# Cross attention of a decoder layer: the second head's sum of weights moved from GpSimd to VectorE in every second block of queries

## The reference, cut to what matters

```python
scores = jnp.einsum('bqhd,bkhd->bhqk', q, k) / TEMP
attn = jax.nn.softmax(scores, axis=-1)
out = jnp.einsum('bhqk,bkhd->bqhd', attn, v).reshape(b, sq, N_HEAD * VALUE_DIM)
out = out @ Wo + bo + residual
```

## Time and profile before

| | |
|---|---|
| median of 3 runs | 1935.51 us |
| all runs | 1913.4, 1935.51, 1937.34 us |
| span of the profiled execution | 1916.1 us |
| mean granted TensorE clock | 0.952 of full speed |
| cross attention, pairs 0 to 7 | from about 640 us to the end |
| one pair, from 1 to 6 | 147.4 us |

### The profile page before, as it was taken

The page is one execution under the profiler, slowest core; times in us unless marked ns, Lnnn a source line. Parts: engine busy times, 40 slices in busy tenths (PEclk is TensorE's granted clock), DMA queues, the critical chain, the costliest instruction groups (busy, mean ns, idle before and its releaser), DMA issues.

```text
span 1916.1 us, 29762 instructions
## 1 busy us (share of the span) xinstructions
PE 1767.4 (92%) x10698; PEld 885.2 (46%) x10698; DVE 1270.0 (66%) x2503; ACT 920.3 (48%) x1866; POOL 940.8 (49%) x800
## 2 busy tenths in 40 slices
PE   7999989998988999999999999999999999999983
PEld 3544444443444544445545545544554554554431
DVE  5677777777643657756656655665665675667888
ACT  2345676666665243344454444445445444445441
POOL 1000000000001466658888888898888888882111
PEclk9867999999999899999999999999999999999996
DMA  4232113332011000000000000000000000000001
GB/s 115 34 37 35 21 16 36 36 45 55 2 34 55 11 0 1 1 11 4 1 11 4 1 10 4 1 11 1 4 11 1 4 1 1 4 11 23 1 28 38
DMA packets 29129, 34.48 MB, mean 18 GB/s; under 512 B 4290, under 2 KB 27139, under 8 KB 27523
## 3 DMA queue, kind: packets, MB, share of 16 engines
q1 hardware_dynamic: 28984, 32.59, 9.1%
HBM read 14.99 MB, written 4.19 MB: 10 GB/s over the span
## 4 chain that ended last, share of the span: by engine, by line
PE 76%; DVE 16%; ACT 4%; issue 3%; SPq 1%; DMA 1%; POOL 0%; ACTq 0%; DVEq 0%; POOLq 0%
PE psum L974 17%; PE psum L954 14%; PE psum L939 9%; DVE maxima L1247 8%; PE psum L860 8%; PE psum L772 6%; PE psum L810 4%; PE psum L835 4%; PE psum L1005 3%; PE psum L927 3%; PE psum L872 2%; PE psum L986 2%; DVE parts_room L1341 1%; DVE stack_room L1297 1%; ACT stack_room L1116 1%
## 5 line engine op out<-in xcount | busy, mean ns | idle before, releaser
L1247 DVE TENSOR_REDUCE maxima<-psum 128x1 f32<-128x400 f32 (+5 forms) x1664 | 860.1, 580 | 322.7 <-PE psum L939 211.7
L747 POOL TENSOR_TENSOR parts_room<-parts_room,weights_room 128x512 f32<-128x512 f32 (+1 forms) x565 | 706.1, 1283 | 136.3 <-ACT weights_room L1137 136.3
L1137 ACT ACTIVATE weights_room<-psum 128x512 f32<-128x512 f32 (+1 forms) x757 | 405.5, 599 | 491.2 <-PE psum L954 429.4
L1065 ACT ACTIVATE weights_room<-psum 128x512 f32<-128x512 f32 (+3 forms) x640 | 300.2, 535 | 183.4 <-PE psum L835 104.1
L1455 POOL TENSOR_SCALAR rstd<-meanvar 128x2 f32<-128x2 f32 (+1 forms) x24 | 9.8, 408 | 726.9 <-DVE meanvar L1197 726.9
L954 PE MATMUL psum<-stack_room,dk_hi 64*128 64x512 f32 (+1 forms) x1408 | 264.1, 410 | 8.1 <-ACT weights_room L1137 4.8
L939 PE MATMUL psum<-k_later,stack_room 64*128 64x400 f32 (+1 forms) x896 | 243.4, 412 | 22.3 <-DVE stack_room L1297 14.6
L939 PEld LDWEIGHTS psum<-k_later,stack_room 64*128 64x128 f32 x896 | 128.4, 184 | 220.8 <-issue 121.2
L974 PE MATMUL psum<-weights_room,parts_room 128*64 128x512 f32 (+1 forms) x754 | 203.1, 606 | 0.0
L974 PE MATMUL psum<-weights_room,late_room 128*64 128x512 f32 (+1 forms) x760 | 202.5, 605 | 0.0
L835 PE MATMUL psum<-stack_room,stack_room 51*128 51x512 f32 (+3 forms) x640 | 143.4, 448 | 34.2 <-DVE maxima L1247 31.7
(11 more groups left out here) (136 smaller groups left out, 1854.4 us busy)
## 6 DMA issues: line engine op xcount, KB each, us to landing
stack_room<-parts_room SPq DMA_DIRECT2D x84, 128.0 KB
x_block<-x_dram SPq DMA_DIRECT2D x8, 512.0 KB, 4.8
x_middle<-x_block SPq DMA_DIRECT2D x4, 512.0 KB, 3.1
x_block<-x_middle SPq DMA_DIRECT2D x4, 512.0 KB, 3.9
out_dram<-x_block SPq DMA_DIRECT2D x8, 256.0 KB, 2.1
stack_room<-parts_room SPq DMA_DIRECT2D x24, 64.0 KB
parts_room<-ctx_dram SPq DMA_DIRECT2D x1, 1536.0 KB
stack_room<-shift_rows SPq DMA_DIRECT2D x64, 2.0 KB
```

The source lines that it names most:

```text
L747: engine.tensor_tensor(sum_[:kw, :], old[:kw, :], weights[u % NP_WEIGHTS][:kw, :], ALU.add) \
L1065: engine.activation(w_self[s % NW][:, m, 0:n], bank_of(use + m)[:, 0:n], ACT.Exp, scale=SELF_SCALE).then_inc(emptied(use + m), 1)
L1137: engine.activation(weights[u % NP_WEIGHTS][:kw, :], pair_scores[u % NSCORES][:kw, :], ACT.Exp, scale=CROSS_SCALE).then_inc(pair_exp, 1)
L1247: engine.tensor_reduce(maxima[:, p % 2, i // TB, n, i % TB, ch:ch + 1], bank_of(use + n)[:, 0:real - k0], AX.X, ALU.max) \
```

## The change

In blocks 1 and 3 of pairs 0 to 6 the adds of the second head (m = 1) are VectorE's; the first head's stay with GpSimd, as do both heads' in blocks 0 and 2. That is 7 pairs x 2 blocks x 12 adds = 168 adds. GpSimd's adds stand at `pair_scores`, VectorE's at `pair_values`, so these adds also come later in the list of stages. The bookkeeping of the two semaphores follows.

```diff
+    def adds_on_vector(p, b, m):
+
+        return on_vector(p) or (b % 2 == 1 and m == 1)
...
         for m in range(HP if added_up(p, j) else 0):
-            made[on_vector(p)] += 1
-            added_made[p, b, j, m] = added_on_vector if on_vector(p) else added_on_pool, made[on_vector(p)]
+            vector = adds_on_vector(p, b, m)
+            made[vector] += 1
+            added_made[p, b, j, m] = added_on_vector if vector else added_on_pool, made[vector]
...
             elif kind == "pair_values":
                 p, b, j, s = at
                 for m in range(HP):
-                    if added_up(p, j) and on_vector(p):
+                    if added_up(p, j) and adds_on_vector(p, b, m):
                         add(dve, engine, p, b, j, s, m)
...
             elif kind == "pair_scores":
                 p, b, j, s = at
                 for m in range(HP):
-                    if added_up(p, j) and not on_vector(p):
+                    if added_up(p, j) and not adds_on_vector(p, b, m):
                         add(pool, engine, p, b, j, s, m)
```

## The result

The changed kernel took 1977.92 us (median of 4 executions, 1976.16 to 1985.25) against 1925.08 us for the kernel before: a ratio of 1.0303, with a 95% interval of 1.0256 to 1.0349. It is slower.

A forecast was written before the change was run, and what follows sets the result against it. TensorE was taken as the bound, waiting only for VectorE. 31 us of adds, 58 with the clash, plus 12 of clock made 70 us; added to the 1935.5 median, 2005 us, 3.6% slower, range 1945 to 2060.

The forecast's parts named there:

- rival 1: VectorE hides the adds except at V4: 20 us, at most 31 without meetings; 1955 to 1967 us, chance 0.27.
- GpSimd's relief: 168 GpSimd adds removed, 215 us of its time, beside TensorE's work and waited for by nobody: 0.
- the clash: VectorE adds meeting GpSimd adds in odd blocks: 0.7 us per two-add stage, raising the sum from 31 to 58 us.
- V4: Values stage of odd blocks between inversions and reductions, without a gap: in pairs 1 to 6 all 1.45 us go to TensorE.
- V3: Values stage of odd blocks, two adds: in pairs 1 to 6 cost 0 in block 1, 1.15 us in block 3.
- The sum without meetings: All odd blocks of pairs 0 to 6, if an add costs what it does in the last pair: 31 us.
- V2: Values stage of block 1, pairs 1 to 6: two adds of 1.45 us fit 2.30 us of idle time, cost 0.
- V5: Values stage of odd blocks, pairs 1 to 6: block 1 0.1 us without meetings, 0.8 with; block 3 0 without.
- V6: Values stage of odd blocks, pairs 1 to 6: cost 0 without meetings, 0.25 us in block 1 with them.
- The clock: One clock dip of 1.7 us in every second of the 14 odd blocks: 12 us, between 0 and 24.
- Rival 2: Every stage pays the full clash: 130 us, with a dip in each block 154; 2065 to 2090 us, chance 0.13.
- the signs that I had named: Profile after: TensorE's waits for VectorE grow from 25 to some 80 us, block 1 of a middle pair 37.7 to 42.

The follow-up runs named there:

- the repeat: The changed kernel measured once more without an edit, against the kernel before: ratio 1.0226 (1.0173 to 1.0279); first copy to last took 1211.2 us.
- the two experiments that split the tiles: Changed kernel with only tiles 4 to 7 of the second head's adds on VectorE, or all but those; first copy to last 1199.2 and 1179.9 us.
- GpSimd's adds short: Changed kernel, GpSimd's first-head adds of odd blocks (tiles 2 to 12) covering only 8 of 512 queries; first copy to last 1199.6 us, against 1167.0 before.
- tiles 4 to 7 only: Changed kernel with only the second head's adds of tiles 4 to 7 of odd blocks on VectorE, 56 for 168; first copy to last 1199.2 us.
- all but these: Changed kernel with tiles 4 to 7 of the second head's adds left to GpSimd, the other 112 on VectorE; ratio 1.0065 (1.0024 to 1.0105).
- a version that is faster than the kernel before: Kernel before, with one inversion per values stage in place of two, in pairs 0 to 5 only; ratio 0.9948 (0.9915 to 0.9982).

## Why the prediction was right

The sign, the place and the mechanism of the largest stall held; the measured 1977.9 us lies in the range of 1945 to 2060, 27 under the 2005 forecast. Of these, 10 us are the median of the kernel before, 1935.5 us when I added to it and 1925.1 with one more execution. The medians differ by 52.8 us (41.3 in the repeat), the change's own part is 43.4 against my 70, and the difference is nearly all in one term. That 1977.9 falls within the band of the forecast itself (1975 to 2040) and not in that of rival 1 (1940 to 1972) is luck: 1925.1 + 43.4 would be 1968.5, and the other 9 us between the medians lie in stretches that the change doesn't touch.

- *GpSimd's relief is worth 0.* Right: even blocks unchanged, GpSimd still out of the chain. Its one new waiter is VectorE, 0.5 us once. But the list of waiters shows only waits by semaphore; the clash makes VectorE wait for GpSimd inside its own instruction, and that stands in no list.
- *V4, 1.45 us, all to TensorE.* Measured 1.52 in block 1, 1.37 in block 3. That it is the place, and not the amount, was shown by the two experiments that split the tiles.
- *V3 hidden in block 1, 1.15 in block 3.* Measured 0 and 0.76.
- *The sum without meetings, 31 us.* With GpSimd's adds short the rest grew by 32.6 us, of which 4.6 are clock (10.0 us lost against 5.4 before, reckoned as below): 28. A few meetings are left in it, since VectorE's adds still meet GpSimd's scaling.
- *The clash, 27 us.* **The mis-sized term.** The fall from 43.4 to 32.6 us puts it at 10.8, and of these 5.4 are clock (15.4 us lost against 10.0): 5.4 us. With one profile of each kernel, whether the clash or the execution brought this clock isn't shown. I had spread meetings evenly over the stages (0.7 us each), as if they fell at random. They don't: in each of the 12 odd blocks of pairs 1 to 6, in both profiles of the changed kernel, V2 takes 2.5 us and V5 2.8 to 2.9, and V3 and V4 take 1.42 or 1.43. GpSimd's adds follow ScalarE's exponentials and VectorE's follow its reductions, and at V3 and V4 VectorE comes first, so that it is GpSimd that waits, if they meet at all. What VectorE loses at V2 and V5 lies ahead of idle time or of a values stage of TensorE; only what V5 hands on to V6 reaches it. Whether GpSimd's times in the trace before, with half its adds taken away, would have told this isn't shown.
- *The clock, 12 us.* In pairs 0 to 6 (1 - granted clock) x length sums to 5.4 us before and 15.4 after, 17.0 in the repeat: 10 to 12 more. I had taken 12. The number of dips differs between two executions of the same kernel, so this agreement is partly luck. The dips fell in block 1 of pairs 1 and 2 and block 3 of pair 5 in one profile, and in block 1 of pairs 1, 3, 4 and 6 in the other, so a stall of 1.5 us sometimes brings one and mostly doesn't. In these seven blocks V6 took 2.4 to 2.6 us, in the other odd blocks of pairs 1 to 6 it took 1.5 to 1.6. In block 1 of pair 1 the dip (granted clock 0.66 from 945 to 950 us) came ahead of V6 (at 952.06), so a dip can bring a meeting, and clash and clock can't be parted cleanly.
- *Missed:* block 3 of pair 6. Its adds of tiles 8 to 11 stand ahead of the reciprocal that starts the fp8 weights' scaling on ScalarE (L1368), which ScalarE awaited for 2.5 us with the exponentials behind it. The block grew by 3.5 us where its like grew by 2.4; the next block is 0.5 us shorter, so about half of the excess is given back. The split by tiles bears this out: with tiles 4 to 7 only the block grew like the other blocks 3 (2.3 us), with all but these it grew by 1.4 where they grew by nothing.
- *Rival 1 (hidden, 20 to 31 us)* was nearer than its chance of 0.27 says: at 43 us for the change alone the case stands nearer to its 31 than to the forecast's 70, and the repeat's interval reaches under 2%. Its arithmetic (V4 and little else, no meetings) gives the 28 us above; what it lacks is the 5 us of clash and the 10 of clock. *Rival 2* (every stage pays the full clash, 3.5 us for two adds) is out: V3 and V4 took 1.42 us, and V5, the longest in the block shown, 2.93.

Of the signs that I had named, TensorE's waits grew to 56 us, not 80, and block 1 of a middle pair to 40.0 or 41.2 us, not 42; both miss by the clash term.

## What to carry to other kernels

Idle time of an in-order engine is worth something only where it stands: lay the added instructions into its timeline at their place in the program, and ask of each what the next instruction behind it releases. Here 8.7 us of work in 14.8 us of idle time cost 2.4 us a block: all of it in block 3, and 1.5 us in block 1, at the places where inversions already stood ahead of a reduction. Before relieving an engine because it is full, look at who waits for it; nobody waited for GpSimd. And where two engines may hold each other up, ask at each place which of them starts first: only the one that comes second pays.

## What the runs showed of the hardware

A VectorE add of two operands in SBUF that meets a GpSimd add takes up to 1.75 us in place of 0.69 if GpSimd's has started before it; if VectorE's has, GpSimd's takes longer. From the timelines of GpSimd and of VectorE in the changed kernel, block 1 of pair 3 and block 3 of pair 3:

```profile
1255.22 1.76 POOL L1498 TENSOR_TENSOR parts_room<-parts_room,parts_room 128x512 f32<-128x512 f32 x1
```

```profile
1311.17 1.75 DVE L752 TENSOR_TENSOR parts_room<-parts_room,parts_room 128x512 f32<-128x512 f32 x1
```

1.76 us of GpSimd against its usual 1.28 is about one VectorE add later; 1.75 against 0.69 is most of a GpSimd add. The second add of this stage, with GpSimd through, takes 0.69. The whole trace sorts by who starts first. Of VectorE's adds in pairs 0 to 6 of the changed kernel 58 start while GpSimd is in an instruction with two operands, and each of them ends 0.55 or 0.56 us after that instruction's end. Another 21 start first and take 0.68 or 0.69 us, and the GpSimd instruction that starts meanwhile takes 1.43 to 1.73. The Trainium skill (SBUF — State Buffer, Who interferes with whom) states that the second to issue waits until the first is done; these durations agree. The product of 5.32 us above and its like of 4.65 us waited longer than that, through a row of four or five GpSimd instructions, and there the measurement goes beyond the rule.

The other surprise is the first stretch of the kernel, self attention, in which all versions run the same instructions (4526 products from the start to the first copy, before and after). From 100 us to the first copy, in the kernel before and in the changed one (TensorE's busy time, then granted clock, DMA share and GB/s):

```profile
100.00:707.34 607.34, 550.99 (x4151) 0.91 0.19 30
```

```profile
100.00:722.32 622.32, 563.17 (x4159) 0.89 0.18 29
```

The end of this stretch lay between 703.28 and 725.70 us in eleven profiles, the latest in a version that is faster than the kernel before. Its granted clock moves with it, 0.91 and 0.89: by (1 - granted clock) x length 55 us are lost in the one and 68 in the other, 13 to 14 us of the 15, as far as two digits of the clock can say. What makes it dip in one execution and not in the next isn't shown. The executions of the kernel before, measured beside the repeat, differ by 35 us, nearly as much as the change is worth: the shortest (1908 us) had a mean granted clock of 0.962, the longest (1943 us) 0.940. So the block lengths of one profile told the versions apart more finely than the medians did.
